# Combining real and imaginary parts of the applied weights on ScalarE, VectorE and GpSimd instead of in the last products

## The reference

```
def _contract_tt(xf, a, b, c, d):
    ac = _c(a)[0]; bc = _c(b); cc = _c(c); dc = _c(d)[..., 0]
    o1 = jnp.einsum('jxk,ky,bcxy->jbcxy', cc, dc, xf)
    return jnp.einsum('oi,icj,jbcxy->boxy', ac, bc, o1)
...
x_ft = jnp.fft.rfft2(x)
out1 = _contract_tt(x_ft[:, :, :MODES1, :MODES2], a1, b1, c1, d1)
out2 = _contract_tt(x_ft[:, :, -MODES1:, :MODES2], a2, b2, c2, d2)
```

## Times and profile before

| | us |
|---|---|
| median of 3 runs | 4960.16 |
| lowest, highest | 4957.18, 4960.85 |
| profiled execution | 4952.49 |
| its span | 4950.7 |
| mean granted TensorE clock of it | 0.977 |

### The profile page before, as it was taken

One profiled execution on the slowest core, in us unless ns is written; L12 is line 12 of the kernel. 1 busy time (PEld: TensorE's weight loads), 2 busy tenths in 40 slices (PEclk: granted clock), 3 DMA queues, 4 the chain that ended last, 5 costly groups with the idle time before them and its releaser, 6 DMA issues. The chain is left out here.

```text
span 4950.7 us, 244841 instructions
## 1 busy us (share of the span) xinstructions
PE 4650.8 (94%) x102182; PEld 3998.5 (81%) x102182; DVE 3450.2 (70%) x5227; ACT 3279.4 (66%) x5782; POOL 3176.7 (64%) x3334
## 2 busy tenths in 40 slices
PE   7999999999999999999997599999999999999999
PEld 6887888888878888888886477777777777779999
DVE  5776777777777677767776777777777777773333
ACT  6767767767677677677773577777777777762332
POOL 6867858858678588577681477777777777760000
PEclk9999999999999999999998799999999999999999
DMA  2132132231321321322324122222222222229999
GB/s 61 56 103 71 56 112 62 58 116 57 90 85 57 107 67 56 108 65 74 100 58 159 41 83 78 78 85 80 81 75 85 80 85 72 85 68 398 420 421 398
DMA packets 609975, 556.27 MB, mean 112 GB/s; under 512 B 16996, under 2 KB 543332, under 8 KB 592612
## 3 DMA queue, kind: packets, MB, share of 16 engines
q1 hardware_dynamic: 609380, 547.21, 33.5%
HBM read 278.71 MB, written 268.44 MB: 111 GB/s over the span
## 5 line engine op out<-in xcount | busy, mean ns | idle before, releaser
L1328 DVE TENSOR_TENSOR Ml<-ring,Mh 128x1024 f16<-128x1024 f32 x832 | 982.3, 1219 | 331.0 <-ACT Mh L1291 325.4
L1291 ACT ACTIVATE Mh<-ring 128x1024 f16<-128x1024 f32 x832 | 810.9, 1024 | 336.5 <-PE ring L1217 336.2
L269 POOL TENSOR_TENSOR A<-Af,A 128x788 f16<-128x788 f32 x512 | 862.7, 1685 | 41.4
L754 DVE SCALAR_TENSOR_TENSOR Y<-ring,Y 128x532 f16<-128x532 f32 x1024 | 682.2, 706 | 279.5 <-ACT Y L607 278.9
L1217 PE MATMUL ring<-wcur,b_hi 64*128 64x128 f16 x16384 | 737.4, 217 | 43.9 <-POOL wcur L1156 39.2
L607 ACT ACTIVATE Y<-ring 128x532 f16<-128x532 f32 x1024 | 575.1, 610 | 270.1 <-PE ring L369 257.1
L1217 PEld LDWEIGHTS ring<-wcur,b_hi 64*128 64x128 f16 x16384 | 614.8, 94 | 146.8 <-DVE Ml L1328 100.7
L1217 PE MATMUL ring<-wcur,b_lo 64*128 64x128 f16 x8192 | 711.6, 217 | 0.0
L369 PE MATMUL ring<-uth,A 64*128 64x138 f16 x12288 | 605.0, 223 | 62.0 <-issue 29.4
L267 POOL CAST A<-Af 128x788 f16<-128x788 f32 x512 | 429.8, 839 | 273.2 <-ACT Af L585 269.0
L769 DVE TENSOR_TENSOR Z<-ring,Z 128x1024 f16<-128x1024 f32 x256 | 313.5, 1225 | 316.4 <-ACT Z L618 316.4
(11 more groups left out here) (156 smaller groups left out, 10777.6 us busy)
## 6 DMA issues: line engine op xcount, KB each, us to landing
xb<-in_x SPq DMA_DIRECT2D x258, 256.0 KB, 2.9
x<-x1b SPq DMA_DIRECT2D x64, 1024.0 KB, 6.3
spec<-sp_out SPq DMA_DIRECT2D x256, 256.0 KB, 3.5
xin<-spec SPq DMA_DIRECT2D x128, 512.0 KB, 3.6
fd<-ft SPq DMA_DIRECT2D x128, 512.0 KB, 4.0
F<-fd SPq DMA_DIRECT2D x64, 1024.0 KB, 20.0
xq<-x SPq DMA_DIRECT2D x64, 1024.0 KB, 16.8
out<-yq SPq DMA_DIRECT2D x64, 1024.0 KB, 18.5
```

Source lines behind the costliest of these rows:

```text
L269: pool.tensor_tensor(lo, Af[:, n], hi, ALU.subtract).then_inc(e_al, 1)
L754: dve.scalar_tensor_tensor(out=Y[:, e, 1, m], in0=ring[:, pr[u], :, 0:UPS], scalar=0.0, in1=Y[:, e, 0, m], op0=ALU.max, op1=ALU.subtract). ...
L1291: act.activation(hi, ps, ACT.Copy).then_inc(e_hi, 1)
L1328: dve.tensor_tensor(lo, ps, hi, ALU.subtract).then_inc(e_lo, 1)
```

## The change

The 32 result columns of one y are two for the high and low part of x (v), times two for its real and imaginary part (r), times 8 images. After the change, the rows of M stand so that partition p and partition p + 64 (or p - 64) hold the real and the imaginary part of the same rank (`unit` and the host's `im`, `rank_i`). ScalarE copies the columns of the imaginary part of x from each half of the partitions to the other (`xt`). VectorE multiplies them with a sign per partition (`sgn`) and adds the columns of the real part, still with v apart (`rt`). GpSimd adds the two values of v (`combine`) to `pout`, which now has one complex result in 128 partitions. So the sum over r is gone from out, `am` is half as large, and apply is handed on in halves of 32 columns of y (a), two banks at a time, instead of quarters.

```
-            dve.tensor_scalar(am[:, :, 0, 0:C], am[:, :, 0, 0:C], alt[:, 0:1], None, ALU.mult)
-            dve.tensor_scalar(am[:, :, 1, 0:C], am[:, :, 1, 0:C], -1.0, None, ALU.mult)
-            dve.tensor_scalar(am[:, :, 1, C:], am[:, :, 1, C:], alt[:, 0:1], None, ALU.mult).then_inc(k_am, 1)
+            dve.tensor_scalar(sgn[:], alt[:], -1.0, None, ALU.mult)
+            dve.tensor_scalar(am[:, :, 0:C], am[:, :, 0:C], alt[:, 0:1], None, ALU.mult).then_inc(k_am, 1)
...
-        pout = sb("pout", [128, 2, 2, B, MODES])
+        pout = sb("pout", [128, 2, B, MODES])
         ft = sb("ft", [128, 2, B, 2, MODES])
-        tmp = sb("tmp", [128, 2, 256])
+        xt = sb("xt", [128, 2, 2 * YQ, 2, B])
+        rt = sb("rt", [128, 2, 2, B, 2 * YQ])
...
-            return (ring[:, UNIT_PAIR[8 * z + u]].rearrange("c k (m y) -> c y k m", y=MODES),
-                    Mh[:, z].rearrange("c y (k m) -> c y k m", k=2)[:, :, :, 8 * u:8 * u + 8],
-                    Ml[:, z].rearrange("c y (k m) -> c y k m", k=2)[:, :, :, 8 * u:8 * u + 8])
+            return (ring[:, UNIT_PAIR[8 * z + u]].rearrange("c k e -> c (k e)")
+                    .rearrange("c (g v y) -> c y v g", v=2, y=MODES),
+                    Mh[:, z].rearrange("c y (v m) -> c y v m", v=2)[:, :, :, 8 * u:8 * u + 8],
+                    Ml[:, z].rearrange("c y (v m) -> c y v m", v=2)[:, :, :, 8 * u:8 * u + 8])
...
+        def applied():
+
+            return ring[:, AUX].rearrange("p k e -> p (k e)").rearrange("p (y v r b) -> p y v r b", v=2, r=2, b=B)
...
                 if n in at and not (first and kind != "app0") and not (last and kind == "app0"):
-                    for j in range(2):
-                        yield kind, 2 * at.index(n) + j
+                    if kind in ("app0", "app1"):
+                        yield kind, at.index(n)
+                    else:
+                        for j in range(2):
+                            yield kind, j
...
+                wait(pool, p_a[z], 2 * s)
...
-            def iteration(s, more=True):
+            def combine(s, z, a):
+                n = 2 * s + a + 1
+                pool.wait_ge(e_r[z], n)
+                carry(pool, carried)
+                pool.tensor_tensor(pout[:, z, :, 2 * YQ * a:2 * YQ * a + 2 * YQ], rt[:, a, 0], rt[:, a, 1], ALU.add
+                                   ).then_inc(e_a[z], 1)
+
+            def iteration(s, more=True, first=False):
                 split(s, 0)
+                if not first:
+                    combine(s - 1, 1, 0)
                 split(s, 1)
+                if not first:
+                    combine(s - 1, 1, 1)
                 if more:
                     pool.wait_ge(p_bld, 32 * s + 16)
                     carry(pool, carried)
                     current(s + 1, 0)
                 convert(s, 1)
                 split(s, 2)
+                for a in range(2):
+                    combine(s, 0, a)
                 if more:
...
+            for a in range(2):
+                combine(MODES - 1, 1, a)
...
-            def apply(s, z, j):
-                if j == 0:
+            def apply(s, z, a):
+                if a == 0:
                     pe.wait_ge(e_lo, len(DIRECT) * s + (6, 13)[z])
                     pe.wait_ge(e_pl, len(POOLED) * s + (2, 3)[z])
                     pe.wait_ge(x_cv[z], s + 1)
-                if j >= 2:
-                    pe.wait_ge(e_a[z], 4 * s + j - 1)
-                elif z == 1:
-                    pe.wait_ge(e_a[0], 4 * s + 3 + j)
-                    pe.wait_ge(e_o1, 2 * s + 1 + j)
                 else:
-                    wait(pe, e_o0, 2 * s - 1 + j)
-                for n in range(YQ):
-                    y = YQ * j + n
-                    o = ring[:, AUX, j % 2, 32 * n:32 * n + 32]
-                    pe.matmul(o, Mh[:, z, y, :], xs[:, z, y].rearrange("p v r b -> p (v r b)"),
-                              start=True, stop=False)
-                    mm = pe.matmul(o[:, 0:16], Ml[:, z, y, :], xs[:, z, y, 0].rearrange("p r b -> p (r b)"),
-                                   start=False, stop=True)
+                    pe.wait_ge(e_r[z], 2 * s + 1)
+                for j in range(2):
+                    if a == 0 and z == 1:
+                        if j == 0:
+                            pe.wait_ge(e_r[0], 2 * s + 2)
+                        pe.wait_ge(e_o1, 2 * s + 1 + j)
+                    elif a == 0:
+                        wait(pe, e_o0, 2 * s - 1 + j)
+                    for n in range(YQ):
+                        y = YQ * (2 * a + j) + n
+                        o = ring[:, AUX, j, 32 * n:32 * n + 32]
+                        pe.matmul(o, Mh[:, z, y, :], xs[:, z, y].rearrange("p v r b -> p (v r b)"),
+                                  start=True, stop=False)
+                        mm = pe.matmul(o[:, 0:16], Ml[:, z, y, :], xs[:, z, y, 0].rearrange("p r b -> p (r b)"),
+                                       start=False, stop=True)
                 mm.then_inc(p_a[z], 1)
             def out(s, z, u, last):
+                pe.wait_ge(e_a[z], 2 * s + 2)
                 if z == 0:
-                    pe.wait_ge(e_a[0], 4 * s + 4)
-                    pe.wait_ge(e_a[1], 4 * s + 3 + u)
+                    pe.wait_ge(e_r[1], 2 * s + 2)
+                elif last:
+                    pe.wait_ge(e_o0, 2 * s + 1 + u)
                 else:
-                    pe.wait_ge(e_a[1], 4 * s + 4)
-                    if last:
-                        pe.wait_ge(e_o0, 2 * s + 1 + u)
-                    else:
-                        pe.wait_ge(e_a[0], 4 * s + 7 + u)
-                for r in range(2):
-                    mm = pe.matmul(ring[:, AUX, u, :], am[:, z, r, C * u:C * u + C],
-                                   pout[:, z, r].rearrange("p b y -> p (b y)"), start=(r == 0), stop=(r == 1))
-                mm.then_inc((p_o0, p_o1)[z], 1)
+                    pe.wait_ge(e_r[0], 2 * s + 4)
+                pe.matmul(ring[:, AUX, u, :], am[:, z, C * u:C * u + C], pout[:, z].rearrange("p b y -> p (b y)"),
+                          start=True, stop=True).then_inc((p_o0, p_o1)[z], 1)
...
-                act.wait_ge(p_a[z], 4 * (s - z) + j + 1)
-                act.activation(tmp[:, j % 2].rearrange("p (m y) -> p m y", y=YQ),
-                               ring[:, AUX, j % 2].rearrange("p (y m) -> p m y", y=YQ)[:, 16:32, :], ACT.Copy
-                               ).then_inc(e_t[z], 1)
+                act.wait_ge(p_a[z], 2 * (s - z) + j + 1)
+                for t in (0, 64):
+                    c = act.activation(xt[t:t + 64, j], applied()[64 - t:128 - t, :, :, 1, :], ACT.Copy)
+                c.then_inc(e_t[z], 1)
...
-                    dve.wait_ge(e_t[z], 4 * (s - z) + j + 1)
-                    dve.tensor_tensor(pout[:, z, :, :, YQ * j:YQ * j + YQ].rearrange("p r b y -> p (r b) y"),
-                                      ps.rearrange("p (y m) -> p m y", y=YQ)[:, 0:16, :],
-                                      tmp[:, j % 2].rearrange("p (m y) -> p m y", y=YQ), ALU.add).then_inc(e_a[z], 1)
+                    dve.wait_ge(e_t[z], 2 * (s - z) + j + 1)
+                    if z == 1:
+                        dve.wait_ge(e_a[0], 2 * (s - 1) + j + 1)
+                    elif not isinstance(s, int) or s > 0:
+                        dve.wait_ge(e_a[1], 2 * (s - 1) + j + 1)
+                    dve.scalar_tensor_tensor(out=rt[:, j].rearrange("p v b y -> p y v b"), in0=xt[:, j],
+                                             scalar=sgn[:, 0:1], in1=applied()[:, :, :, 0, :], op0=ALU.mult,
+                                             op1=ALU.add).then_inc(e_r[z], 1)
...
-    swap = np.concatenate([np.arange(64), np.arange(64, 128) ^ 1])
+    at = np.arange(128)
+    v, unit, h, i = at // 64, at // 8 % 8, at // 4 % 2, at % 4
+    rank_i, im = 32 * h + 4 * unit + i, v ^ h
...
-        ri, ir = np.concatenate([a[0], a[1]], axis=1), np.concatenate([a[1], a[0]], axis=1)
-        am.append(np.stack([np.stack(p, axis=1).reshape(128, 2 * C) for p in ((ri, ir), (ir, ri))], axis=1)[swap])
+        am.append(np.concatenate([a[im, rank_i], a[1 - im, rank_i]], axis=1))
...
-        "alt": np.tile(np.array([[1.0], [-1.0]], np.float32), (64, 1))[swap], "iy": f32(iy), "ix": f32(dfth.T),
+        "alt": f32(1.0 - 2.0 * im[:, None]), "iy": f32(iy), "ix": f32(dfth.T),
```

More of the change, by code:

```diff
@@ L892, in phase2, with factors @@
         w_lo = sb("w_lo", [128, 2, MODES, 2, MODES], F16)
[L893 to L898, removed]
+        am = sb("am", [128, 2, 2 * C])
+        sgn = sb("sgn", [128, 1])
+        factors(nc, bst_d, cst_d, dst_d, am_d, alt_d, b_hi, b_lo, w_hi, w_lo, am, sgn)
+        modes(nc, spec, b_hi, b_lo, w_hi, w_lo, am, sgn, fd)
+def factors(nc, bst_d, cst_d, dst_d, am_d, alt_d, b_hi, b_lo, w_hi, w_lo, am, sgn):
     with ExitStack() as ctx:
@@ L1057, in _, with modes @@
                     dve.tensor_copy(w[t:t + 64, :, :, 1, :], w[64 - t:128 - t, :, :, 0, :])
-def modes(nc, spec, b_hi, b_lo, w_hi, w_lo, am, fd):
```

(14 more changed lines are left out.)

## The result

The changed kernel takes 4916.6 us, the median of four runs (4911.75 to 4917.35), against 4960.5 us of the kernel before on the same chip (4957.18 to 4961.36): a ratio of 0.991, with an interval of 0.989 to 0.993. It is faster, by 44 us where 128 were forecast. It lies 44 us above the forecast's own range (4797 to 4873) and 7 us above the 80% range (4785 to 4910). The profiled execution took 4916.3 us, its span 4914.2.

What follows compares the result with a forecast made beforehand. TensorE was taken to set the pace. Its 21.95 us an iteration without waits plus 2.0 us of waits gave 23.95 against 25.97; over 63 iterations 127 us, plus 1 us of preparation, giving 4832 us (range 4797 to 4873).

Steps and rivals of the forecast that it cites:

- TensorE's removal: Out groups lose the r loop, four of eight records in each of two groups: 3.44 us less an iteration.
- The mechanism: TensorE waits for apply's serial chain (xt copies, then rt): 0.65 us twice an iteration, about 0.05 at app1 and out0.
- The new order of M's rows: In the build units, PSUM reads go from steps of 256 to 512 bytes, priced at nothing.
- the price of VectorE's instruction: In apply, rt's scalar_tensor_tensor of 512 elements, written in 128-byte steps, takes 0.75 us; upper bound 1.41 us.
- signs of being wrong: Listed observations against the forecast; for VectorE's apply instruction, rt at 1.2 us or more.
- the second rival: VectorE's stepped rt write takes 1.41 us: 26.3 us an iteration, 4982 us; chance dearer 0.13, of which slower 0.06.
- the pair of xt copies: ScalarE's two copies in apply's chain: 0.49 us to the second's start, then 0.60 us.
- VectorE's queue: Behind the shorter out1, unit 3 waits 0.3 us; unit 11 waits for unit 8, 0.3 us.
- the floor of 21.95: Middle-stage iteration time in us if TensorE never waited: 25.97 - 3.44 - 0.58.
- rival 4: TensorE's gaps lower the middle stage's clock by 2%: 30 us lost, 4862 us; chance in full 0.05.
- rival 3: GpSimd becomes the bound through its combine adds: at 1.3 us each, 24.9 us an iteration, 4892 us; chance 0.05.
- Start and tail: The stage's start and end: fewer products but a longer serial chain at the end, left at zero.

Runs made afterwards that it cites:

- e2: Changed kernel with one xt copy of 128 partitions instead of two of 64, leaving out the exchange of halves: 4831.3 us, ratio 0.976 to the kernel before.
- e1: Changed kernel with rt written packed, in the order in which VectorE reads: 4852.9 us, ratio 0.981 to the kernel before.
- e4: Changed kernel with the first app0 group after unit 10 instead of 11: 4845.5 us, ratio 0.980 to the kernel before.
- e3: Changed kernel with rt's PSUM operand read packed (wrong columns added), its write still in steps: 4904.4 us, ratio 0.991 to the kernel before.
- e5: Changed kernel with both packed rt and the first app0 group after unit 10: 4826.6 us, ratio 0.974 to the kernel before.
- e12: Changed kernel with xt copies cut by columns, two of 128 partitions and 256 elements, halves not exchanged: 4842.9 us, ratio 0.977 to the kernel before.
- e9: Changed kernel with every out product made twice: 5134.0 us, ratio 1.035 to the kernel before.
- e11: Changed kernel with GpSimd's combine done twice: 5017.3 us, ratio 1.012 to the kernel before.
- e10: Changed kernel with packed rt, first app0 group after unit 10, and a one-operand copy replacing GpSimd's add: 4809.1 us, ratio 0.970 to the kernel before.

## Why the prediction failed

**TensorE's removal** held: 3.44 us an iteration less. A group of output products went from 3.70 us to 1.98, twice an iteration.

**The mechanism** held. The waits came where they were forecast, before app0's second pair and before out1, released by rt, and one copy fewer (e2), packed output (e1) and a third unit (e4) each shorten them. The chain was laid out rightly; its terms were too small. The new order of M's rows cost nothing, as priced: Ml takes 1.217 us against 1.219.

**The step that failed is the price of VectorE's instruction**: "I take 0.75, because ScalarE and VectorE pay nothing for steps elsewhere". It measured 1.107 us. The rows behind that sentence are reads the earlier trace rows, as the prediction itself said against its rival; a write in steps of 128 bytes stood in none. (The read that gave GpSimd's factor goes in steps of 512 bytes from value to value by the source, `xin[128, 2, B, 2, MODES]` read along B, and not of 256.) The bounds were 0.68 and 1.41 us, and the value lies in the upper half. e1 and e3 together put all of the excess on the write. It is worth 0.71 us an iteration, 45 us over 63. None of the signs of being wrong was set for it: they began at 1.2 us. The Trainium skill (SBUF — State Buffer, the note on cachelines in "Door 1: The DMA port swizzle") pointed the right way; the factor is 1.48 on VectorE, not the 1.89 of GpSimd's stepped read the earlier trace rows, and so the second rival came true by half, and not as far as slower.

**The second mis-sized term is the pair of xt copies**, 0.49 + 0.60 in the chain. The overlap was read from instructions on 128 partitions and carried to 64, where it is absent: 0.605 from start to start. That is 0.12 us in each of four chains, and with rt it lengthens each by 0.47 us. Four times that is 1.9 us; the waits for rt grew by 3.07 - 1.4 = 1.67.

**The third is VectorE's queue**, 2 x 0.3. The longer chain gives VectorE time, so these waits were 0.18 us together in the changed kernel. With rt at its forecast price (e1) they came out at 0.39 and 0.47, with 0.07 more at units 0 to 2. The parts add up: 3.07 and 0.18 against 1.4 and 0.6 makes 1.25 us more, less the 0.09 by which the floor of 21.95 lies above the sum of its stretches, 16 x 0.705 + 4 x 1.69 + 2 x 1.91 = 21.86. That gives 25.11 in place of 23.95.

**The clock**, rival 4, came true in small. Before, the granted clock was always 1.00 from the fourth iteration to the last; now the upper level gives way to the lower every 126 us for 3.4 us (13 times), and lengthens that iteration by 0.75 us: 10 us in all. Ahead of each fall TensorE had waited twice per iteration for about 1 us. Apart from one to three falls at the stage's ends, which the kernel before has too, there were none with waits of 0.62 us twice (e1) or one of 0.9 to 1.0 (e4, e5), 2 with one of 1.05 (e2, e12), and 19 and 52 with more and longer ones (e9, e11). That the waits cause them is what this pattern suggests; no run changed the clock alone.

**GpSimd**, rival 3, was not the bound: 0.728 us a combine against 0.67, and 22.4 us an iteration as forecast. It is near: e10 shows that it costs e5 0.27 us an iteration, and e11 that four more sums cost 1.7.

**Start and tail** were left at zero. The first and last distances are 4.4 us longer, and 3.1 us come back behind the last. The first group of output products comes 5.0 us later, but that isn't shown to be the change: in the other runs it comes anywhere from 2802.6 to 2825.2 us. Nor can the 1 us forecast for the preparation be seen in that scatter.

In numbers: 127 us forecast; 61 x 0.702 = 42.8 gained and 6 lost. Of the 84 us that the iterations fell short, rt's write is 45 by the undisturbed iterations of e1 and the clock 10. The 29 left are 63 x 0.45, the 24.40 us of e1 against the 23.95 forecast. By the table, 0.22 of that 0.45 stands in the waits for rt and 0.33 in VectorE's queue, less the 0.09. How much of it the copies' missing overlap causes stays open: no run restores the overlap and keeps all else. It is a coincidence that 63 x 4 x 0.12 = 30 comes near.

## What to carry to other kernels

Before pricing an elementwise instruction by a row of the same size, look for one that agrees in the direction of the stepped operand and in its partitions: a read in steps is no evidence for a write, and an instruction on half of the partitions may take the full time and overlap with nothing. When a change shortens the full engine, the chain behind its buffers decides. Each link counts in full in the waits for that chain, but a shorter link can let a wait on another queue come out, which here took back half. Write the links packed, and try the order of the work again, which here was worth as much as the change. When two edges of a range are far apart and a stated rule speaks for the dear one, take a value between them.

## What the runs showed of the hardware

- VectorE, 512 fp32 values by 128 partitions, one operand in PSUM: 0.747 us with packed output, 1.107 with values 128 bytes apart, and 1.106 with that output and a packed read.
- ScalarE, two copies in a row: 1.19 us for two of 0.59 on 64 partitions (512 elements), the same crossed or not; 1.13 us for two of 0.61 on 128 (512 elements); 0.66 us for two of 0.38 on 128 (256 elements).
- GpSimd: the sum of two fp32 operands of 256 elements takes 0.728 us, a copy of the same 0.399.
- The granted clock fell for 3.4 us every 126 us (13 times) in the changed kernel, whose TensorE waits 1.09 and 0.99 us in each 25.1, and not once in the middle of the stage with two waits of 0.62 us in 24.4 (e1).
